# A graph attention layer's last 27 edge tiles as one softmax chunk in place of chunks of 16 and 11

## What is computed

```
edge_emb = edge_attr_full @ ew.T + eb
xw = x @ W
xj = xw[src].reshape(-1, H, D) + edge_emb.reshape(-1, H, D)
alpha = leaky_relu(einsum(xi, att_i) + einsum(xj, att_j), 0.2)
amax = segment_max(alpha, dst)
ea = exp(alpha - amax[dst])
denom = segment_sum(ea, dst)
msg = xj * (ea / (denom[dst] + EPS))[..., None]
aggr = segment_sum(msg, dst)
return aggr.mean(axis=1) + b
```

## Time and profile before

| | us |
|---|---|
| median of the timed runs | 3387.27 |
| the profiled execution, first to last instruction | 3764.7 |
| POOL busy | 2210.5 (59%) |
| PE busy | 2439.0 (65%) |
| DVE busy | 2004.0 (53%) |
| ACT busy | 696.7 (19%) |
| first gather of layer 0 | 475.5 after the start |
| first gather of layer 1 | 1133.2 |

### The profile page before, as it was taken

How to read it: one execution, slowest core, us unless ns; L and a number is a source line. 1 busy time by engine, 2 the same in 40 slices (tenths; PEclk the granted TensorE clock), 3 DMA queues, 4 the chain that set the end, 5 groups by cost and what they waited for, 6 DMA issues and landing times.

```text
span 3764.7 us, 48376 instructions
## 1 busy us (share of the span) xinstructions
PE 2439.0 (65%) x13595; PEld 2001.4 (53%) x13595; DVE 2004.0 (53%) x6216; ACT 696.7 (19%) x3102; POOL 2210.5 (59%) x2357
## 2 busy tenths in 40 slices
PE   6779726666582766658276665837576582766668
PEld 6679615555461655547165554725455461655546
DVE  8955624554472555547255554725454472555456
ACT  0078511111121111112111111211111121111112
POOL 0067466666626766662666666266676626666661
PEclk8555555555565555556555555655555565555556
DMA  3212122222202222221222222022222202222221
GB/s 101 97 60 80 30 52 54 53 52 57 49 24 51 54 51 53 56 49 30 47 54 52 53 56 49 25 53 54 50 53 57 50 24 50 54 50 53 52 49 40
DMA packets 114121, 195.78 MB, mean 52 GB/s; under 512 B 39897, under 2 KB 77272, under 8 KB 113864
## 3 DMA queue, kind: packets, MB, share of 16 engines
q0 software_dynamic: 62560, 130.25, 15.2%
q1 hardware_dynamic: 51304, 62.42, 5.3%
HBM read 180.86 MB, written 11.67 MB: 51 GB/s over the span
## 4 chain that ended last, share of the span: by engine, by line
DVE 36%; PE 25%; another core or an unknown queue 20%; issue 13%; DVEq 3%; POOL 1%; ACT 1%; ACTq 1%; DMA 0%; POOLq 0%
PE bank L745 10%; PE bank L747 6%; DVE acc L1200 4%; DVE into L1143 2%; DVEq L1016 2%; PE bank L718 2%; DVE pw L1161 2%; DVE alpha L1094 2%; PE bank L741 2%; PE bank L783 2%; DVE fwd L1150 2%; DVE lanes L1129 2%; DVE prod L1072 1%; PE bank L766 1%
## 5 line engine op out<-in xcount | busy, mean ns | idle before, releaser
L510 POOL DMA_INDIRECT ring<-table,srci x1955 | 1941.2, 993 | 937.6 <-issue 556.4
L745 PE MATMUL bank<-pw,ring 128*128 128x48 f32 x3910 | 1210.9, 404 | 203.3 <-issue 201.8
L745 PEld LDWEIGHTS bank<-pw,ring 128*128 128x128 f32 x3910 | 1014.9, 314 | 302.9 <-issue 231.1
L1200 DVE TENSOR_TENSOR acc<-acc,bank 128x288 f32 x490 | 222.8, 455 | 1128.7 <-remote 857.3
L747 PE MATMUL bank<-onehot,est 128*36 128x24 f32 x3910 | 632.6, 243 | 222.9 <-issue 221.7
L741 PE MATMUL bank<-zeros 128*128 128x288 bf16 x490 | 208.5, 426 | 697.1 <-DVE pw L1161 438.7
L747 PEld LDWEIGHTS bank<-onehot,est 128*36 128x36 f32 x3910 | 391.2, 149 | 393.9 <-issue 226.6
L741 PEld LDWEIGHTS bank<-zeros 128*128 128x128 bf16 x490 | 55.4, 113 | 752.0 <-DVE pw L1161 453.3
L586 ACT ACTIVATE dd<-dd 128x66 f32<-128x66 f32 x75 | 19.4, 258 | 2163.4 <-DVE dd L1154 1177.9
L580 ACT COPY ai_win<-ai_rows 128x48 f32 x1955 | 336.3, 229 | 432.6 <-issue 410.5
L491 POOL TENSOR_TENSOR ring<-ring,acc 128x512 f32<-128x512 f32 x98 | 117.1, 1195 | 250.1 <-ACT ring L545 246.7
(11 more groups left out here) (214 smaller groups left out, 2610.1 us busy)
## 6 DMA issues: line engine op xcount, KB each, us to landing
ring<-table,srci POOLq DMA_INDIRECT x1955
ai_rows<-lo_dram SPq DMA_DIRECT2D x28, 896.0 KB, 4.3
at<-in_attr SPq DMA_DIRECT2D x65, 224.0 KB
table<-ring SPq DMA_DIRECT2D x15, 390.0 KB, 3.5
table<-ring SPq DMA_DIRECT2D x5, 325.0 KB, 3.4
result<-ring SPq DMA_DIRECT2D x24, 64.0 KB
x_mid<-ring SPq DMA_DIRECT2D x3, 384.0 KB, 2.7
table<-ring SPq DMA_DIRECT2D x5, 130.0 KB, 2.4
```

Source lines behind the costliest of these rows:

```text
L510: nc.gpsimd.indirect_dma_start(out=ring[:, slot(t), :], out_offset=None, in_=table, in_offset=bass.IndirectOffsetOnAxis(ap=srci[:, t:t + 1 ...
L745: nc.tensor.matmul(wide[:, 0:H, at_k], ring[:, slot(t), 0:D], pw[:, g % DEEP, k, :, :], start=False, stop=False, skip_group_check=True)
L1200: V.tensor_tensor(win, win, grp_sum(g).rearrange("p (r w) -> p r w", r=REG), ALU.add)\
```

## The change

The last two chunks of each layer, of 16 and 11 tiles, become one of 27. All that depends on the number of chunks follows: 14 chunks a layer, the last with seven groups (six of four tiles and one of three, so 98 groups as before), one chain and one rescale fewer on DVE, one window pass and one exponential fewer on ACT, one attribute load fewer on SP, two row blocks in place of three in the preparation. By `chain_at`, the chain of the last chunk now runs beside chunk 12 alone, with its scan after group 2.

```diff
-CH = [K] * 13 + [16, 11]
+CH = [K] * 13 + [27]
...
-        ROW_BLOCKS = [(0, 13, K), (13, 14, CH[13]), (14, 15, CH[14])]
+        ROW_BLOCKS = [(0, 13, K), (13, 14, CH[13])]
```

## The result

| | before | after |
|---|---|---|
| median of the timed runs, us | 3387.84 (3385.08 to 3389.48) | 3423.09 (3421.13 to 3426.59) |
| first to last instruction of the profiled execution, us | 3764.7 | 3421.1 |

The change makes the kernel slower: the ratio of the times is 1.0106, with a 95% interval of 1.0092 to 1.012, or 35 us (31 to 41). It was forecast at 3418 us.

The account below looks back on a forecast made before the run. Timed run bound by back-to-back gathers; the last chunk's scan waits for gather 390, 7.6 us a layer, 38 in five, or 17 with PE lag; 31 taken: 3387.3 + 31 = 3418 us, range given 3384 to 3432.

Parts of the forecast that it names:

- Bound of the timed run: Whole layers: timed run bound by gathers back to back, 1.30 us each; profiled run bound differently where the change is made.
- sum: Whole kernel before: 475.5 us to first gather, 5 x (507 + 29.7), 4 x 42.0, and 38.5: 3366 us.
- The points of time: Layer's end: chunk 13 starts 11.3 to 14.0 us after chunk 12's chain may begin.
- G: The end of a layer's last gather, from which the forecast counts times at the layer's end.
- The gain that was to be lost: Layer's end: without chunk 14's chain, PE's gap of 3.6 us before chunk 14 goes.
- faster rival: Sparse stretches also in timed run, gather 390 landed in time: gain 5 to 18 us, 3376 us; chance 0.12.
- The term that was mis-sized: Layer's end: PE's lag, at most 4.3 us a layer, could cut the 7.6 us a layer lost by waiting for gather 390.
- sparse stretches: About one a chunk in the profile before: PE starts single matmuls 2.8 us apart; 59 us of gather waits in layer 0.
- The forecast's own mark: Whole kernel: a profile shorter than before beside timed runs longer than before.
- Before the layers: Preparation: 12 of 36 row loads and some flag work go; between 0 and -5.4 us, taken as 0.
- no change: Layer's end: PE's timed lag is 7.6 us a layer give or take 1.4; about 3387 us, chance 0.10.
- Slower by more: Layer's end: PE at its higher clock shortens groups but not DVE's chain; loss up to 45 us, no separate chance.

Follow-up runs that it names:

- before_again: The kernel before, unchanged, run for a second profile: 3388.36 us, with a span of 3386.4 us.

## Why the prediction was right, point by point

*Bound of the timed run.* Right, and the reading on which all hung: the profiled execution and the timed run were bound differently where the change is made. It was argued from the 377 us between span and median and from a sum that came within 21 us of the median; before_again shows it. The page of the Trainium skill that spoke for the rival, "NOTIFIC — the notification-queue block", section "Constraints, capacities, measured rates", says that records cost an engine no cycles. What this case shows is less: 48376 records stand in a span of 3764.7 us and 48376 in one of 3386.4, so their number alone does not stretch an execution; one without records was not set beside them. What did not follow is that the stretches were then the kernel's own. Whether the section on overflow names their cause is not shown by any run here, and stays open.

*The points of time.* Chunk 12 at G - 21.1 (measured -21.2 in before, -21.6 in after), landing 1.7 us (1.9), chain 12.3 us for 27 tiles (12.1), chunk 13 at G + 14.0 (14.0), the last add at G + 37.3 (37.3) and before at G + 29.7 (29.6): all of the forecast values were worked out from rows of the stretched execution, by taking only durations and distances from stretches in which the engine concerned waited for nobody.

*The gain that was to be lost.* The prediction put it at 3.6 us of gap, and in its faster rival at 1.1 to 3.4 us a layer. The kernels without the last 11 gathers show 3.8 to 4.1: 3.6 of it the gap (chunk 12's start to last add 50.8 us in before, 47.2 in after). The other 0.5 is no gain of the end: chunk 12 starts 13.8 us after its own last gather in both, but the 16 gathers that follow take 21.7 us in after and 21.1 in before, and the point from which I count comes later by that. The larger operations cost nothing on the path, as long as DVE has the slack.

*The term that was mis-sized.* The 21 us between sum and median were taken as possible lag of PE, which would have hidden up to 4.3 of the 7.6 us a layer; for that reason 38 was cut to 31. There is no lag at the end of a layer. What was short is the 1.30 us for one gather. In the second profile of before, the gather phase of layer 0 is 510.9 us where the sum had 507: 392.0 of gathers (389.4 in the sum) and 118.9 of pauses (117.3), 114.3 listed as "issue" and 4.6 as "PE bank"; the latter are fifteen pauses of 0.30 us as well, and no gather waits for a ring slot. In the mean of the five layers the phase is 4.1 us longer than in the sum. Five times 4.1 is 20.5, and 2.0 lie around the span. The sum without the cut, 38, is what the traces show from G to the last add (38.1). The timed difference of 35 (31 to 41) holds it. The 9 to 15 us that the Trainium skill puts around a kernel ("Runtime: NRT & Kernel Launch", "The ~15µs preamble/postamble breakdown") are not in this measurement: timed time and span of the same execution differ by 1.8 to 2.0 us in the nine later profiles (3422.88 and 3421.1 for after). The figure was rightly left out of the sum.

*What the profile after was to show.* Here it was wrong. I expected the sparse stretches again, a span of 3745 to 3770 us, and the wait visible only in part. The span is 3421.1, and the wait stands open in all five layers. The forecast's own mark, a profile shorter than before beside timed runs longer than before, came true, but for another reason than I had in mind: both profiles would have been disturbed in my picture, and only one was.

*Before the layers.* Taken at nothing; the first gather is at 475.6 us in after and at 475.5 to 475.7 in before. Right.

*The rivals.* Both fell with the timed result. Before_again shows why: the faster one wanted chunk 12 at G - 1.9 to G - 5.7 and no change at G - 15 to G - 12, and it starts at G - 21.2. Slower by more did not show: the clock of PE is 0.50 from G to the last add in both kernels.

## What to carry to other kernels

Before any row of a profile is used, hold its span against the timed median: here they differed by 11%, and the profile's critical chain was not that of the timed run. When work is chunked behind a stream of transfers, the last chunk begins one landing and one chain after the very last transfer, so its size is what the end pays for; cut the last chunks so that each is ready about when the one before it ends (24, 16, 15 here), and let their number be what it comes to. A chain fewer is worth something only where nothing else is waited for: 3.8 us a layer at this end with the last 11 gathers left out, nothing in the middle.

## What was not expected of the hardware

*One execution of a kernel can be 378 us longer in its profile than another.* In layer 0, 56 us of it are in the gather phase and 19 between G and the last add; they come from stretches in which PE starts single matmuls 2.8 us apart with nothing to wait for the earlier trace rows. The spans of the nine later profiles all stand 1.8 to 2.0 us under the time of their execution. The cause is open, and so is whether that execution was long itself, since its timed duration is not on record.

*A layer's end can be 3.3 us shorter in one layer.* From the last add to the next layer's first gather all layers of all profiles here take 41.7 to 42.3 us, but layer 1 of after takes 38.8. DVE is full in that stretch. The groups of DVE and GpSimd in 15 us of it, of after, first layer 0 and then layer 1:

```profile
L1072 DVE CUSTOM_DVE_ANT_0 prod<-ring,vrow,v 128x128 f32<-128x128 f32 x26 | 10.5, 404 | 0.0
...
L517 POOL TENSOR_TENSOR S<-S 128x128 f32<-128x128 f32 x13 | 5.9, 454 | 5.0 <-ACT S L590 5.0
```

```profile
L1072 DVE CUSTOM_DVE_ANT_0 prod<-ring,vrow,v 128x128 f32<-128x128 f32 x29 | 10.5, 362 | 0.0
...
L517 POOL TENSOR_TENSOR S<-S 128x128 f32<-128x128 f32 x15 | 9.4, 629 | 1.2
```

In that stretch of layer 0 six of the 26 L1072 on DVE take 0.62 to 0.63 us, the others 0.33 to 0.34; in that of layer 1 all 29 take 0.35 to 0.38, and GpSimd's L517 takes 629 ns in place of 454 instead. The ten profiles hold forty such ends between two layers. In 39 of them eleven of the fifty L1072 take over 0.6 us and no L517 does; in the one that is shorter no L1072 does and 21 of the 25 L517 do. Eleven times 0.29 us is 3.2, about what that end is shorter, and in after each of the long L1072 starts within 0.03 us of an L517. So the two engines seem to hinder one another, and which of them pays differs. That is a reading of traces; no run tested it.
